# Scan layer of a vision tower: nine y tiles solved inside the loop, y and h statistics shared with ScalarE, five tiles kept in PSUM

## What is computed

```python
def scan_dir(z, Wp):                      # h_t = delta_t * h_{t-1} + gate_t
    o = z @ Wp
    delta, gate = sigmoid(o[..., :d]), o[..., d:] * z
    ...
z   = xn @ W_in                           # xn = layernorm(h)
out = concat(scan_dir(z, W_fwd), reversed scan_dir(z, W_bwd)) @ W_out
y   = out + xn
h   = h + (y - mean(y)) * rsqrt(var(y) + 1e-5) * gamma + beta
...                                       # then ffn0 on layernorm(h)
```

## Time and profile before

| | |
|---|---|
| median of three runs | 1547.92 us |
| time of the profiled execution itself | 1549.41 us |
| its span, first to last instruction | 1547.6 us |
| TensorE busy | 1385.4 us, 90% of the span |
| VectorE busy | 832.9 us, 54% |
| ScalarE busy | 378.7 us, 24% |
| GpSimd busy | 483.6 us, 31% |

### The profile page before, as it was taken

The page is one execution under the profiler, slowest core; times in us unless marked ns, Lnnn a source line. Parts: engine busy times, 40 slices in busy tenths (PEclk is TensorE's granted clock), DMA queues, the critical chain, the costliest instruction groups (busy, mean ns, idle before and its releaser), DMA issues.

```text
span 1547.6 us, 21953 instructions
## 1 busy us (share of the span) xinstructions
PE 1385.4 (90%) x6469; PEld 1078.2 (70%) x6470; DVE 832.9 (54%) x1692; ACT 378.7 (24%) x738; POOL 483.6 (31%) x350
## 2 busy tenths in 40 slices
PE   0586939999999999389998989999999989999997
PEld 0584427888444444147776778888888879999996
DVE  8985898555222222663657765555555543333332
ACT  3114133121111111242223312333332212222221
POOL 0651530450344443001111035533323213343332
PEclk9999969999999999699999999999999999999999
DMA  4592007103955554600000504666665679676443
GB/s 102 112 153 24 1 22 266 34 10 116 342 93 89 89 94 62 195 22 1 1 0 1 185 21 133 204 215 209 216 224 200 222 272 372 208 206 187 75 74 42
DMA packets 88403, 197.04 MB, mean 127 GB/s; under 512 B 28256, under 2 KB 32224, under 8 KB 84832
## 3 DMA queue, kind: packets, MB, share of 16 engines
q1 hardware_dynamic: 68240, 154.20, 30.8%
q0 software_dynamic: 20096, 42.02, 14.7%
HBM read 112.24 MB, written 81.02 MB: 125 GB/s over the span
## 4 chain that ended last, share of the span: by engine, by line
PE 80%; DVE 11%; issue 3%; DMA 2%; ACT 2%; POOLq 1%; POOL 0%; DVEq 0%; SPq 0%; ACTq 0%
PE ps L1616 25%; PE ps L1676 19%; PE ps L1738 9%; PE ps L2143 6%; PE ps L1764 4%; PE ps L442 4%; PE ps L1706 2%; PE ps L555 2%; DVE held L495 1%; PE ps L1752 1%; PE ps L2112 1%; PE ps L2168 1%; PE ps L861 1%; PE ps L862 1%; DVE held L1383 1%
## 5 line engine op out<-in xcount | busy, mean ns | idle before, releaser
L1676 PE MATMUL ps<-moe_rounded 128*128 128x384 f32 (+2 forms) x1800 | 375.3, 351 | 0.0
L1676 PEld LDWEIGHTS ps<-moe_rounded 128*128 128x128 f32 x1800 | 326.9, 188 | 33.4
L1383 DVE SCALAR_TENSOR_TENSOR held<-ps,moe_scratch,held 128x512 f32<-128x512 f32 (+1 forms) x255 | 187.4, 747 | 180.0 <-PE ps L1616 179.2
L1616 PE MATMUL ps<-moe_expert_parts,moe_rows_parts 128*128 (+1 forms) x1320 | 256.5, 347 | 3.1 <-DVE moe_rows_parts L1407 1.5
L1616 PE MATMUL ps<-moe_rounded 128*128 128x512 f32 (+3 forms) x885 | 241.8, 393 | 11.8 <-DVE moe_rounded L1365 9.7
L1616 PEld LDWEIGHTS ps<-moe_expert_parts,moe_rows_parts 128*128 128x128 f32 (+1 forms) x1320 | 217.5, 188 | 16.3 <-issue 4.1
L1616 PEld LDWEIGHTS ps<-moe_rounded 128*128 128x128 f32 (+2 forms) x885 | 146.5, 171 | 50.7 <-DVE moe_rounded L1365 12.0
L1393 DVE TENSOR_TENSOR moe_scratch<-moe_scratch,ps 128x256 f32<-128x256 f32 (+1 forms) x80 | 37.7, 471 | 237.4 <-ACT moe_scratch L1598 237.4
L1738 PE MATMUL ps<-moe_experts,moe_scratch 128*128 x320 | 144.2, 593 | 0.6 <-issue 0.6
L1487 POOL TENSOR_TENSOR moe_split_parts<-moe_scratch,moe_split_parts 128x704 fp32r<-128x704 f32 (+2 forms) x48 | 88.8, 1855 | 172.8 <-ACT moe_split_parts L1580 172.8
L1471 POOL DMA_INDIRECT slot_tokens<-moe_scratch x68 | 73.5, 1081 | 173.2 <-DVE held L1383 165.9
(11 more groups left out here) (315 smaller groups left out, 1690.1 us busy)
## 6 DMA issues: line engine op xcount, KB each, us to landing
moe_expert_parts<-expert_parts SPq DMA_DIRECT2D x8, 3840.0 KB, 13.0
expert_parts<-moe_split_parts SPq DMA_DIRECT2D x32, 704.0 KB
moe_scratch<-in_ffn_gate_up SPq DMA_DIRECT2D x32, 352.0 KB, 4.3
xn_rows<-moe_xn SPq DMA_DIRECT2D x2, 4096.0 KB, 13.0
moe_experts<-in_ffn_gate_up SPq DMA_DIRECT2D x8, 1024.0 KB, 15.5
expert_parts<-moe_split_parts SPq DMA_DIRECT2D x8, 1024.0 KB
moe_scratch<-in_ffn_sh_gate_up SPq DMA_DIRECT2D x15, 512.0 KB, 3.5
tokens<-sb SPq DMA_DIRECT2D x16, 256.0 KB
```

The lines of the kernel that those rows point to most:

```text
L1383: v.scalar_tensor_tensor(out=hb[0:rows, t, :], in0=ps[0:rows, ADDED[t % 3], :], scalar=sg[0:rows, t:t + 1], in1=hb[0:rows, t, :], op0=ALU. ...
L1616: mm = t.matmul(out, lhs(k, x), rhs(k, y), start=(k == 0 and i == 0), stop=(k == ks - 1 and i == 2))
L1676: mm = t.matmul(unit_banks(u, m)[j], weights(k, x, j), xT[y][:, k, unit_cols(m)], start=(k == 0 and i == 0), stop=(k == KD - 1 and i == 2))
```

## The change

- `KEPT` goes from 7 to 5: twelve tiles are lent, five stay in PSUM. The class-token tile moves from place 8 to place 9 of the order.
- The statistics of seven y tiles (places 1, 3, 5, 7, 10, 12, 14) are taken by ScalarE: a Copy with accumulator for the mean, a small Copy that makes the bias, a Square with accumulator for the variance.
- rstd of the first nine tiles is solved inside the loop (turn 10), that of the other eight behind it. ScalarE scales the lent tiles from the first solve on, between its statistics.
- Three h statistics (lent tiles 0 to 2) move into turns 14 to 16 of the loop. Those of h tiles 3 to 6 are taken by ScalarE in the same three steps.
- The aggregations and the solve of the next layer's norm stand at the end of the scan layer's list, with 13 aggregations; `norm.solve` goes out of ffn_layer.
- GpSimd adds beta in the order in which xn is made, each tile as soon as its xn is written, instead of after all of them.
- In the tokenizer two semaphores become one (`ker` is folded into `arg`, whose waits count one more).

```diff
-    YORDER = list(range(8)) + [NB] + list(range(8, NB))
+    YORDER = list(range(9)) + [NB] + list(range(9, NB))
-    KEPT = 7
+    KEPT, FIRST = 5, 9
+    Y_BY_SCALAR = [YORDER[i] for i in (1, 3, 5, 7, 10, 12, 14)]
+    ROOT = float(D) ** -0.5
+    H_BY_SCALAR = (3, 4, 5, 6)
...
         def y_gamma(n):
-            v.wait_ge(norm.sem, aggr_at[n])
+            if n in Y_BY_SCALAR:
+                v.wait_ge(yst, 3 * Y_BY_SCALAR.index(n) + 3)
+            else:
+                v.wait_ge(norm.sem, aggr_at[n])
...
+        IN_LOOP = {14: 0, 15: 1, 16: 2}
         for i in range(T + 2):
-            if i < T:
+            if i < T and YORDER[i] not in Y_BY_SCALAR:
                 y_stats(YORDER[i])
-            if 1 <= i <= T:
+            if 1 <= i <= T and YORDER[i - 1] not in Y_BY_SCALAR:
                 y_mean(YORDER[i - 1])
+            if i == FIRST + 1:
+                c.wait()
+                v.wait_ge(yst, 3 * len([n for n in Y_BY_SCALAR if n in lent[:FIRST]]))
+                norm.newton(v, c, norm.mv[:, 0:FIRST, 1], 1.0, LN_EPS, slice(0, FIRST))
+                y_solved.append(c.base + c.n)
             if i >= 2:
                 y_gamma(YORDER[i - 2])
+            if i in IN_LOOP:
+                lent_stats(IN_LOOP[i])
+                c.n += 1
         c.wait()
-        norm.newton(v, c, norm.mv[:, :, 1], 1.0, LN_EPS)
-        norm.closed(c)
+        v.wait_ge(yst, 3 * len(Y_BY_SCALAR))
+        norm.newton(v, c, norm.mv[:, FIRST:T, 1], 1.0, LN_EPS, slice(FIRST, T))
...
         h_own(0)
-        h_own(1)
-        own_stats(0)
...
+        for k in range(1, KEPT):
+            h_own(k)
+            own_stats(k - 1)
+            lent_stats(FREED - KEPT + k - 1)
+        own_stats(KEPT - 1)
+        lent_stats(FREED - 1)
+        c.n += 2 * KEPT
+        c.wait()
+        for t in range(T):
+            if t not in H_BY_SCALAR:
+                r = tile_rows(t)
+                c.put(v.bn_aggr(norm.mv[0:r, t, :], norm.stats[0:r, t, :]))
+        c.wait()
+        v.wait_ge(yst, 3 * (len(Y_BY_SCALAR) + len(H_BY_SCALAR)))
+        norm.newton(v, c, norm.mv[:, :, 1], 1.0, LN_EPS)
...
     def gpsimd(p):
         p.wait_ge(w_fb, 16 * 7)
-        p.wait_ge(xr, T - len(BY_SCALAR))
-        p.wait_ge(xa, len(BY_SCALAR))
-        for n in YORDER:
+        for n in ORDER:
             r = tile_rows(n)
+            if n in BY_SCALAR:
+                p.wait_ge(xa, BY_SCALAR.index(n) + 1)
+            else:
+                p.wait_ge(xr, 1 if n == NB else n // 2 + 2)
             p.tensor_tensor(hb[0:r, n, :], hb[0:r, n, :], bet[0:r], ALU.add).then_inc(hbr, 1)
...
+        def y_stats(k):
+            n = Y_BY_SCALAR[k]
+            y = ps[:, y_bank(n), :]
+            s.wait_ge(outp, YORDER.index(n) + 1)
+            s.activation(yb[:, n, :], y, ACT.Copy, scale=1.0 / D, accum_out=norm.mv[:, n, 0:1]).then_inc(yst, 1)
+            s.wait_ge(yst, 3 * k + 1)
+            s.activation(nmr[:, n:n + 1], norm.mv[:, n, 0:1], ACT.Copy, scale=-ROOT).then_inc(yst, 1)
+            s.wait_ge(yst, 3 * k + 2)
+            s.activation(yb[:, n, :], y, ACT.Square, bias=nmr[:, n:n + 1], scale=ROOT, accum_out=norm.mv[:, n, 1:2]).then_inc(yst, 1)
...
+        for k in range(5):
+            y_stats(k)
+        for k in range(FIRST):
+            scaled(k)
+            if k in (1, 4):
+                y_stats(5 + k // 4)
+        h_stats(0)
+        h_stats(1)
+        for k in range(FIRST, FREED):
+            scaled(k)
+        h_stats(2)
+        h_stats(3)
...
     def vector(v):
-        if made is None:
-            norm.solve(v)
```

More of the change, by code:

```diff
@@ L149, in tokenizer @@
     dch = sem("tok_vector_chain")
-    ker = sem("tok_decay_args")
-    arg, sines = sem("tok_sine_args"), sem("tok_sines")
+    arg, sines = sem("tok_powers_then_sine_args"), sem("tok_sines")
     tabr = sem("tok_tables_ready")
@@ L248, in vector @@
         ktf = kt.rearrange("p g k -> p (g k)")
-        v.scalar_tensor_tensor(out=ktf, in0=kc[:, 1, 0:NK], scalar=pos[:, 0:1], in1=kc[:, 0, 0:NK], op0=ALU.mult, op1=ALU.add).then_inc(ker, 1)
+        v.scalar_tensor_tensor(out=ktf, in0=kc[:, 1, 0:NK], scalar=pos[:, 0:1], in1=kc[:, 0, 0:NK], op0=ALU.mult, op1=ALU.add).then_inc(arg, 1)
         k24 = bc(kt.unsqueeze(2), 2, HH)
@@ L284, in spread @@
             return bc(x.unsqueeze(2), 2, w)
-        v.wait_ge(ker, 1)
+        v.wait_ge(arg, 1)
         c.put(v.tensor_tensor(m, k24, along(fhi), ALU.mult))
@@ L394, in scalar @@
     def scalar(s):
-        s.wait_ge(ker, 1)
+        s.wait_ge(arg, 1)
         for g in range(NG):
@@ L400, in scalar @@
         for n, (sine, cosine) in enumerate(((im, re), (sm[4], sm[3]))):
-            s.wait_ge(arg, n + 1)
+            s.wait_ge(arg, n + 2)
             s.activation(sine, sine, ACT.Sin, scale=-TWO_PI).then_inc(sines, 1)
@@ L600, in scan_layer @@
     hbr, hr, tch = sem("scan_h_plus_beta"), g.h_ready, sem("scan_scaled_y")
-    ctr = sem("scan_centred_y")
+    ctr, yst = sem("scan_centred_y"), sem("scan_stats_by_scalar")
     def z_of(q):
@@ L680, in y_gamma, with lent_stats @@
             y = ps[0:r, y_bank(n), :]
-            v.wait_ge(norm.sem, aggr_at[n])
+            if n in Y_BY_SCALAR:
+                v.wait_ge(yst, 3 * Y_BY_SCALAR.index(n) + 3)
+            else:
+                v.wait_ge(norm.sem, aggr_at[n])
             v.scalar_tensor_tensor(out=y if n in own else yb[0:r, n, :], in0=y, scalar=norm.mv[0:r, n, 0:1], in1=gam[0:r], op0=ALU.subtract, op1=ALU.mult).then_inc(yr, 1)
+        def lent_stats(k):
+            v.wait_ge(tch, k + 1)
+            norm.take_stats(v, hb, lent[k])
+        IN_LOOP = {14: 0, 15: 1, 16: 2}
         for i in range(T + 2):
-            if i < T:
+            if i < T and YORDER[i] not in Y_BY_SCALAR:
                 y_stats(YORDER[i])
-            if 1 <= i <= T:
+            if 1 <= i <= T and YORDER[i - 1] not in Y_BY_SCALAR:
                 y_mean(YORDER[i - 1])
+            if i == FIRST + 1:
[3 more added lines that the diff above has]
+                y_solved.append(c.base + c.n)
             if i >= 2:
                 y_gamma(YORDER[i - 2])
+            if i in IN_LOOP:
+                lent_stats(IN_LOOP[i])
+                c.n += 1
         c.wait()
-        norm.newton(v, c, norm.mv[:, :, 1], 1.0, LN_EPS)
-        norm.closed(c)
-        y_solved.append(norm.count)
+        v.wait_ge(yst, 3 * len(Y_BY_SCALAR))
+        norm.newton(v, c, norm.mv[:, FIRST:T, 1], 1.0, LN_EPS, slice(FIRST, T))
+        y_solved.append(c.base + c.n)
         v.wait_ge(hbr, T)
@@ L705, in own_stats @@
             norm.take_stats(v, hb, own[k])
-        def lent_stats(k):
-            v.wait_ge(tch, k + 1)
-            norm.take_stats(v, hb, lent[k])
         h_own(0)
-        h_own(1)
-        own_stats(0)
[L714 to L720, removed]
+        for k in range(1, KEPT):
[13 more added lines that the diff above has]
+        norm.newton(v, c, norm.mv[:, :, 1], 1.0, LN_EPS)
+        norm.closed(c)
     def zero(p):
@@ L784, in scalar, with scaled, h_stats @@
             delta(c)
-        s.wait_ge(norm.sem, y_solved[0])
-        for n in lent:
+        def y_stats(k):
[7 more added lines that the diff above has]
+            s.activation(yb[:, n, :], y, ACT.Square, bias=nmr[:, n:n + 1], scale=ROOT, accum_out=norm.mv[:, n, 1:2]).then_inc(yst, 1)
+        def scaled(k):
+            n = lent[k]
+            s.wait_ge(yr, k + 1)
+            s.wait_ge(norm.sem, y_solved[0 if k < FIRST else 1])
             r = tile_rows(n)
             s.activation(yb[0:r, n, :], yb[0:r, n, :], ACT.Copy, scale=norm.rstd[0:r, n:n + 1]).then_inc(ctr, 1)
+        def h_stats(j):
+            n = H_BY_SCALAR[j]
+            done = 3 * (len(Y_BY_SCALAR) + j)
+            s.wait_ge(tch, n + 1)
+            s.activation(yb[:, n, :], hb[:, n, :], ACT.Copy, scale=1.0 / D, accum_out=norm.mv[:, n, 0:1]).then_inc(yst, 1)
+            s.wait_ge(yst, done + 1)
+            s.activation(nmr[:, n:n + 1], norm.mv[:, n, 0:1], ACT.Copy, scale=-ROOT).then_inc(yst, 1)
+            s.wait_ge(yst, done + 2)
+            s.activation(yb[:, n, :], hb[:, n, :], ACT.Square, bias=nmr[:, n:n + 1], scale=ROOT, accum_out=norm.mv[:, n, 1:2]).then_inc(yst, 1)
+        for k in range(5):
[10 more added lines that the diff above has]
+        h_stats(3)
     def tensor(t):
```

## The result

The changed kernel takes 1544.27 us (median of 15 executions, 1541.29 to 1548.33) against 1547.31 for the kernel before (15 executions, 1543.61 to 1550.33): a ratio of 0.9978, with an interval of 0.9970 to 0.9986. That is 3.0 us less; 2.8 were forecast. The prediction's bound of 0.2% lies inside the interval, so the result does not say on which side of it the change is. It allows 2.2 to 4.6 us less.

What follows compares the result with a forecast made beforehand. Behind the last y tile TensorE idles 23.5 us while VectorE is busy throughout. The terms -5.64 - 0.28 + 0.85 + 0.7 + 1.6 = -2.8 us take 1547.92 to 1545.1, range 1543.8 to 1546.5.

Steps and rivals of the forecast that it cites:

- bound of 0.2%: Whole kernel: the difference the measurement can tell, 3.1 us, with limits at 1544.8 and 1551.0 us for faster and slower.
- h work behind the last tile, 15.13 us: VectorE behind the last y tile: two fewer tiles from PSUM and seven fewer statistics take out 5.64 us.
- 13 aggregations instead of 17: VectorE behind the last y tile: four fewer aggregations at 0.07 save 0.28 us.
- later start of the second solve: End of the y loop: moved h statistics make VectorE start the solve at 199.4 instead of 198.56, 0.85 us lost.
- the ninth addition stalls it: Second y solve at 199.4: it waits for GpSimd's ninth lent addition, +0.7 us, between 0 and 1.4.
- beta additions make the last xn group late: First norm: five early beta additions delay VectorE's last solve by 5.3 us, leaving +1.6 us, between 0 and 5.6.
- The price that the diff does not show: First norm and second y solve: VectorE's small operations wait for GpSimd's additions, costing 1.6 + 0.7 us.
- Work moved into the loop: In the y loop: the added first solve costs nothing near 185.5 us; the moved h statistics are not wholly free.
- (a): Rival: no stall in the first norm, the rest stands; 1542.8 to 1543.5 us; chance 0.2.
- (b): Rival: dearer stalls, several additions inside the second solve and slow ones in the first norm; 1546.5 to 1548.5 us; chance 0.17.
- (c): Rival: ScalarE's y statistics over 3 us a tile make gammas wait and hold TensorE's banks; 1546.5 to 1548; chance 0.05.
- (d): Rival: a gap of about 2 us near 152 us drops TensorE to its slower rate; 1553 us; chance 0.06.

Runs made afterwards that it cites:

- e3: The changed kernel, with GpSimd's ninth lent addition held back until the second y solve is done; 1544.38 us in one execution.
- e1: The changed kernel, with beta added only after all of xn, as before the change; 1544.09 us, ratio 0.9981 to the kernel before.
- e2: The kernel before, with only the early additions of beta put in; 1549.58 us, ratio 1.0019.
- e5: The changed kernel, with all y statistics on VectorE again; 1544.55 us in one execution.
- e4: The changed kernel, with the three h statistics taken behind the y loop instead of inside it; 1548.40 us in one execution.
- e6: The changed kernel with both e1 and e3: beta late and the ninth addition held; 1542.66 us, ratio 0.9974.
- e7: e6 with the statistics of six h tiles instead of four on ScalarE; 1541.59 us, ratio 0.9965.

## Why the prediction was right

Each term against its row of the table, before to changed:

| term | predicted | measured |
|---|---|---|
| h work behind the last tile, 15.13 us | -5.64 | -5.79 (9.34) |
| 13 aggregations instead of 17 | -0.28 | -0.26 (1.25 to 0.99) |
| later start of the second solve | +0.85 | +0.72 (0.15 + 0.57) |
| the ninth addition stalls it | +0.7 | +0.57; +0.64 by e3 |
| beta additions make the last xn group late | +1.6 | +1.16, by e1 and e2 too |
| sum | -2.8 | -3.6 in the stretch |

**The price that the diff does not show** was there, and it is the term that was mis-sized. Its mechanism held: the fifth addition was to end between 146.1 and 146.8 and ended at 146.48, or 145.98 without the 0.5 us by which the stretch starts later; four or five operations were to have gone by then, and the fifth began at 146.54; ScalarE was to start its three tiles at 147.5, and started at 147.75, or 147.25 without the same 0.5. Counted from the z tile ScalarE was 2.44 us late instead of 2.7, and its slack hid 1.28 of that instead of 1.1: hence 1.16 for 1.6. The prediction's own terms give 1.5 (5.35 - 2.66 - 1.17), not 1.6.

Two things it did not have. It let the last solve begin at 140.17 and put the whole delay into it; in fact 1.48 of the 5.27 us arose ahead of it, in one operation of the third group's solve and one xn tile. That the total came out as the foreseen 5.3 is no accident, since the end of the fifth addition sets it either way. And it took ScalarE's slack as fixed, while with faster first z products ScalarE comes sooner and the same additions cost 1.57 us (e5).

**The stall of the second solve** began as foreseen, with one operation of 0.80 (0.9 was named), and e3 shows that the ninth addition is its cause. e4 shows the case that the prediction gave as its upper bound, two additions still to come: two operations are stalled, and the solve takes 2.99 - 1.82 = 1.17 us more than without a stall (e3); 1.4 was the bound.

**Work moved into the loop** cost what was worked out. The first solve, at 186.81 us, ran where VectorE was ahead and left nothing on the path: the whole loop takes 29.95 us against 29.80, and this 0.15 is what the prediction gave to the h statistic beside the last tile (195.99 against 195.84). e4 puts the value of the three moved statistics at 1.60 us.

**The rivals.** (a) No stall in the first norm: its mechanism is refuted by the rows at 142.86 to 145.31. (b) Dearer stalls: no; the two cost 1.16 + 0.57 = 1.73 us where 2.3 had been taken. (c) ScalarE late: its y tile takes 1.73 us (1.8 estimated), and no gamma waits for it:

```profile
171.34 0.60 ACT L813 ACTIVATE sb<-ps 128x512 f32<-128x512 f32 x1 [3.05 <-PE ps L920]
...
172.88 0.19 ACT L817 ACTIVATION_READ_ACCUMULATOR sb<-ps,sb 128x1 f32 x1
```

(d) Slower multiplications behind ScalarE's delay: TensorE did stand for 1.22 us before 153.75, and the eight multiplications behind it kept their pace of 3.60:

```profile
153.75 0.63 PE L554 MATMUL ps<-held,sb 128*128 128x128 f32 x4 [1.22 <-ACT sb L562]
154.22 3.60 PE L854 MATMUL ps<-sb 128*128 128x512 f32 x8
```

**What stays open.** The stretch gives 3.6 us. The two timed comparisons have 3.0 and 3.5 us between their medians, and cannot tell these from 3.6. That the first of them lies nearer to the forecast 2.8 than the stretch does is chance. The times of e1 and e2 stand 1.5 and 1.1 us above what their stretches say; part of e1's goes with the clock groups, and for e2's nothing was found.

## What to carry to other kernels

Ask of every edit to GpSimd's list which chain of small VectorE operations it will now run beside: the edit that starts beta earlier saved nothing and cost 1.16 us or more, because such a chain pays up to one addition at each step that meets one, here four of nine steps. Where a chain ends a stage, hold the other engine's work back until it is done, as e3 and e6 do; and when work is then taken out ahead of a held result, look where its consumer now stands, or part of the gain turns into a wait, as in e7; moving the consumer to the end of the list suggests itself and was not tried. Terms below a microsecond are to be read from a stretch between two fixed points of the trace, here repeatable to 0.03 us in two executions with equally slow first z products, since the whole time scatters by some microseconds; and the start of the stretch has to be checked for what differs ahead of it.

## What the runs showed of the hardware

GpSimd's 128x512 addition and VectorE's smallest operations alternate whole: three operations in a row took 1.19 to 1.20 us beside additions of 1.24 (6.19 for five), with one input (line 529) as with two (lines 531 and 532). A longer one is hit as well: of the eight xn tiles that VectorE writes (line 543), each 128x512 with one input tile in SBUF, the longest takes 1.50 us in the changed kernel and 0.54 in the kernel before. Bn statistics and `h_own`, whose input is in PSUM, kept their 0.6 us beside additions. The Trainium skill, "SBUF — State Buffer", Who interferes with whom, says that the one of the two engines that issues first has the shared pair of ports for its whole instruction and the other is blocked; the durations here agree. What I had not expected is how regularly the two take turns: a chain pays one addition at every step that meets one, not one in all. The scans are hit too. Before the change, with beta additions beside them, they took up to 2.33 us; in the changed kernel, once GpSimd is done:

```profile
160.33 1.22 DVE L656 TENSOR_TENSOR_SCAN sb<-sb 64x516 f32<-64x516 f32 x1
161.59 1.23 DVE L658 TENSOR_TENSOR_SCAN sb<-sb 64x516 f32<-64x516 f32 x1
```

This did not move the first y tile (16.26 us from ScalarE's table load to it in both kernels), so the scans did not set that time.

The first eight z multiplications took 5.74 and 5.96 us in the profiles before and after, 3.70 in those of e1, e5 and e7, which run the same list up to there on TensorE, and 5.37 to 6.12 in the other five. The granted clock does not show it. The windows of the changed kernel and of e1, with TensorE's busy time and, after it, the granted clock (1.00, the level of 2.4 GHz), both show it full:

```profile
132.90:136.50 3.60, 3.58 (x5) 1.00 0.00 0
```

```profile
132.90:136.50 3.60, 3.50 (x8) 1.00 0.00 0
```

The pace changes within the slow group: in the changed kernel the fifth product starts at 136.50 and the sixth at 137.35, 0.85 us apart, and the last three take 1.53 us together; in the later groups, at 3.60 for eight, they start 0.43 apart. What sets it I did not find.
